# Softmax shift through one 24-column transpose and three row transfers, auxiliary ring of five tasks

## The reference

```python
xn = _layernorm(x, axis=-1)
s = _L0_attn_ref(xn, ...)          # softmax over keys, floored at 1e-10, times v, out projection
g = _silu(_L0_ffn_ref(xn, ...))    # router top-4, silu(gate)*up, down, plus a shared expert
x = x + s * g
```

## Time and profile before

| | |
|---|---|
| median of three runs | 728.79 us (726.35 to 729.39) |
| the profiled execution | 730.4 us, span 728.2 us |
| PE busy / VectorE / ScalarE / POOL | 634.6 / 485.3 / 462.1 / 331.5 us |
| DMA engines' mean busy share, queue of SP | 30.9% |
| transposes of the shift (L764) | 256 |
| copies of the shift (L1227) | 32 |

### The profile page before, as it was taken

How to read it: one execution, slowest core, us unless ns; L and a number is a source line. 1 busy time by engine, 2 the same in 40 slices (tenths; PEclk the granted TensorE clock), 3 DMA queues, 4 the chain that set the end, 5 groups by cost and what they waited for, 6 DMA issues and landing times.

```text
span 728.2 us, 18937 instructions
## 1 busy us (share of the span) xinstructions
PE 634.6 (87%) x5458; PEld 449.4 (62%) x5458; DVE 485.3 (67%) x973; ACT 462.1 (63%) x1082; POOL 331.5 (46%) x691
## 2 busy tenths in 40 slices
PE   2299699966899989999999899899989999998992
PEld 1194256943666666666666666666667666766651
DVE  5939742036777688677777867867787777775265
ACT  1532752036887777787777778777777887785311
POOL 5600677774344433444454344344434444543124
PEclk9979898556999999999999999999999999999996
DMA  8970465500034333333433323333332333321562
GB/s 258 148 245 0 139 160 143 132 0 13 28 82 99 93 80 74 77 82 82 95 89 84 73 73 83 82 83 85 103 74 73 78 82 82 78 55 30 194 201 86
DMA packets 76852, 69.45 MB, mean 95 GB/s; under 512 B 15938, under 2 KB 67204, under 8 KB 76820
## 3 DMA queue, kind: packets, MB, share of 16 engines
q1 hardware_dynamic: 68596, 60.51, 30.9%
q0 software_dynamic: 8224, 8.54, 6.4%
HBM read 47.88 MB, written 21.17 MB: 95 GB/s over the span
## 4 chain that ended last, share of the span: by engine, by line
PE 65%; DVE 14%; ACT 9%; issue 7%; DMA 3%; SPq 0%; ACTq 0%; POOL 0%; DVEq 0%; POOLq 0%
PE PSB L721 8%; PE PSB L696 7%; PE PSB L822 7%; PE PSB L814 6%; PE PSB L740 6%; PE PSB L786 5%; PE PSB L796 5%; PE PSB L743 5%; DVE NEGM L1216 4%; ACT PB L984 4%; ACT PSB L975 3%; PE PSB L670 3%; PE PSB L655 2%; PE PSB L642 2%; PE PSB L672 2%
## 5 line engine op out<-in xcount | busy, mean ns | idle before, releaser
L1216 DVE TENSOR_REDUCE NEGM<-PSB 128x1 f32<-128x1024 f32 (+7 forms) x256 | 192.1, 753 | 65.5 <-PE PSB L698 64.6
L984 ACT ACTIVATE PB<-PSB 128x128 f32<-128x128 f32 (+7 forms) x256 | 165.9, 649 | 39.5 <-PE PSB L723 34.3
L975 ACT ACTIVATE PSB<-PSB,NEGM 128x1024 f32<-128x1024 f32 (+7 forms) x256 | 182.9, 714 | 11.7 <-DVE NEGM L1216 10.7
L1222 DVE TENSOR_SCALAR PB<-PB 128x128 f32<-128x128 f32 (+7 forms) x256 | 118.9, 473 | 60.0 <-ACT PB L984 56.1
L721 PE MATMUL PSB<-STACKS 111*128 111x512 bf16 (+3 forms) x384 | 105.7, 330 | 20.4 <-ACT PSB L975 12.4
L696 PE MATMUL PSB<-STACKS 111*128 111x512 bf16 (+3 forms) x384 | 109.9, 343 | 10.3 <-ACT PSB L975 9.6
L1427 POOL DMA_INDIRECT slot_table<-XE,DI x64 | 66.6, 1040 | 60.3 <-DVE DI L1193 41.1
L1483 POOL DMA_INDIRECT moe_rows<-YE,IDX x32 | 52.9, 1654 | 45.6 <-issue 45.6
L740 PE MATMUL PSB<-PB,VH 128*32 128x256 f32 x640 | 67.3, 383 | 0.0
L743 PE MATMUL PSB<-PB,VH 128*32 128x128 f32 x1024 | 61.5, 276 | 0.0
L721 PEld LDWEIGHTS PSB<-STACKS 111*128 111x128 bf16 x384 | 29.4, 98 | 50.6 <-ACT PB L984 20.5
(11 more groups left out here) (189 smaller groups left out, 1344.6 us busy)
## 6 DMA issues: line engine op xcount, KB each, us to landing
STACKS<-q_parts SPq DMA_DIRECT2D x192, 32.0 KB
STACKS<-k_parts SPq DMA_DIRECT2D x192, 32.0 KB
WG<-in_L_ffn_w_gate_dram SPq DMA_DIRECT2D x32, 176.0 KB
WU<-in_L_ffn_w_up_dram SPq DMA_DIRECT2D x32, 176.0 KB
WD<-in_L_ffn_w_down_dram SPq DMA_DIRECT2D x32, 176.0 KB
q_parts<-PB SPq DMA_DIRECT2D x8, 384.0 KB, 2.6
k_parts<-PB SPq DMA_DIRECT2D x8, 384.0 KB, 3.1
XN<-in_L_attn_qkv_dram SPq DMA_DIRECT2D x4, 512.0 KB, 6.2
```

What stands on the lines that cost most here:

```text
L975: act.activation(sc, sc, ACT.Exp, bias=NEGM[:, par, i:i + 1], accum_out=LSUM[:, par, i:i + 1]).then_inc(exp1_done, 1)
L984: act.activation(PB[:, k % 2, prob_offset(s):prob_offset(s) + (s + 1) * P], psf[:, base:base + (s + 1) * P], ACT.Exp).then_inc(exp2_done, 1)
L1216: dve.tensor_reduce(NEGM[:, par, i:i + 1], psf[:, base:base + (i + 1) * P], AX_X, ALU.max, negate=True).then_inc(max_ready, 1)
L1222: dve.tensor_scalar(p, p, FLOOR, None, ALU.max).then_inc(clamp_done, 1)
```

## The change

1. The shift's parts are stored part by part, `C3[P, 3, NQ]`. One transpose of 24 columns (a 128 x 24 operand) puts 24 rows of 128 into columns 256 and up of `O_BANK`, at step 5 instead of step 7; it waits for the chain, for the copy before it and for the heads' evacuation.
2. VectorE copies them into a new tile `CT[24, 128]` at step 5 (`turn_shift`), and three transfers on SP's queue (`store_shift`), each from eight partitions of 256 bytes into one row of 2 KB, put them into the query stack. They stand at the end of SP's work for a unit. `c_rows_ready` counts 48 per unit.
3. The ring has five tasks, SA, TR, GU, SB, DN. SA stays at steps 2 and 3, TR moves from step 1 to step 3 (ScalarE's copy from step 2 to step 4), GU from steps 4 and 5 to 5 and 6, SB's part 0 from 6 to 7, DN stays. ScalarE's and VectorE's part of GU moves from step 6 to 7, the evacuation of heads from 4 to 3.
4. `values` also waits for the copy of the shift, POOL's chain for that copy instead of the rows, and `DST2` shares the space of `PK`.

```diff
-TR, SA, GU, SB, C, DN = range(6)
-AUX_TASKS = 6
+SA, TR, GU, SB, DN = range(5)
+AUX_TASKS = 5
+C_COL = 256
...
-        C3 = sb("C3", [P, NQ, 3], BF16)
+        C3 = sb("C3", [P, 3, NQ], BF16)
+        CT = sb("CT", [3 * NQ, P], BF16)
...
                 store_heads(it, k - 1)
+                store_shift(it, k + 1)
+
+            def store_shift(it, k):
+
+                hold(sp, c_turned, unit(it, k, 1, 1))
+                rows = QS[k % SLOTS]
+                for a in range(3):
+                    sp.dma_start(rows[SHIFT + a:SHIFT + a + 1, :].rearrange("o (t q) -> o t q", q=P),
+                                 CT[NQ * a:NQ * a + NQ, :]).then_inc(c_rows_ready, 16)
...
+            store_shift(0, 0)
+            store_shift(0, 1)
...
-                    pe.wait_ge(c_rows_ready, unit(it, k, 1, 1))
+                    pe.wait_ge(c_rows_ready, unit(it, k, 48, 48))
...
+                    pe.wait_ge(c_turned, UNITS if is_last(it, k) else unit(it, k, 1, 2))
...
-            def c_transpose(o, ready, parts_count):
-
-                pe.wait_ge(c_parts_ready, parts_count)
-                for i in range(NQ):
-                    ins = pe.transpose(o[SHIFT:SHIFT + 3, i * P // 2:(i + 1) * P // 2].bitcast(BF16),
-                                       C3[:, i, :], IDB[:, :])
-                ins.then_inc(ready, 1)
+            def c_transpose(it, k):
+
+                pe.wait_ge(c_parts_ready, unit(it, k, 1, 1))
+                if k >= 1:
+                    pe.wait_ge(c_turned, unit(it, k))
+                    pe.wait_ge(o_evacuated, unit(it, k, 1, -1))
+                pe.transpose(PSB[0:3 * NQ, O_BANK, C_COL:C_COL + P // 2].bitcast(BF16),
+                             C3[:, :, :].rearrange("p a t -> p (a t)"), IDB[:, :]).then_inc(c_flipped, 1)
...
-                    if s == 1:
-                        if not first:
-                            expert_down(it, k - 1, *aux_begin(it, k - 1, DN))
-                        expert_transpose(it, k, *aux_begin(it, k, TR))
-                    if s == 7 and not last:
-                        c_transpose(*aux_begin(it, k, C), unit(it, k, 1, 2))
-                    if s in (2, 3):
-                        shared(it, k, SA, s - 2, last)
-                    if s in (4, 5):
-                        expert_up(it, k, s - 4, last)
-                    if s == 6:
-                        shared(it, k, SB, 0, last)
+                    if s == 1 and not first:
+                        expert_down(it, k - 1, *aux_begin(it, k - 1, DN))
+                    if s in (2, 3):
+                        shared(it, k, SA, s - 2)
+                    if s == 3:
+                        expert_transpose(it, k, *aux_begin(it, k, TR))
+                    if s == 5 and not last:
+                        c_transpose(it, k + 1)
+                    if s in (5, 6):
+                        expert_up(it, k, s - 5)
+                    if s == 7:
+                        shared(it, k, SB, 0)
...
-                    if s == 2:
-                        o = aux_task(it, k, ix(TR))
+                    if s == 4:
+                        shared(it, k, SA)
+                        o = aux_task(it, k, TR)
                         act.activation(XET[:, :, :].rearrange("p c m -> p (c m)"), o[:, 0:D], ACT.Copy)\
                             .then_inc(xet_ready, 1)
-                    if s == 4:
-                        shared(it, k, ix(SA), SA)
-                    if s == 6:
-                        tanh_gate(it, k, ix(GU), GU, FE)
+                    if s == 7:
+                        tanh_gate(it, k, GU, FE)
...
-                dve.wait_ge(aux_ready[b], count)
-                dve.tensor_copy(QS[k % SLOTS][SHIFT:SHIFT + 3, :], PSB[SHIFT:SHIFT + 3, AUX + b, :].bitcast(BF16))\
-                    .then_inc(c_rows_ready, 1)
+            def turn_shift(it, k):
+
+                dve.wait_ge(c_flipped, unit(it, k, 1, 1))
+                if k >= 1:
+                    dve.wait_ge(c_rows_ready, unit(it, k, 48))
+                dve.tensor_copy(CT[:, :], PSB[0:3 * NQ, O_BANK, C_COL:C_COL + P // 2].bitcast(BF16))\
+                    .then_inc(c_turned, 1)
```

More of the change, by code:

```diff
@@ L745, in values, with aux_begin @@
                 ins.then_inc(pv_done, 1)
[L747 to L752, removed]
+            def aux_begin(it, k, task):
+                if task >= 2:
+                    pe.wait_ge(*aux_done(it, k, task - 2))
                 elif k >= 1:
[L754 to L757, removed]
+                    pe.wait_ge(*aux_done(it, k - 1, task + AUX_TASKS - 2))
+                b, _ = aux(it, k, task)
                 return PSB[:, AUX + b, :], aux_ready[b]
-            def c_transpose(o, ready, parts_count):
-                pe.wait_ge(c_parts_ready, parts_count)
-                for i in range(NQ):
-                    ins = pe.transpose(o[SHIFT:SHIFT + 3, i * P // 2:(i + 1) * P // 2].bitcast(BF16),
-                                       C3[:, i, :], IDB[:, :])
-                ins.then_inc(ready, 1)
+            def c_transpose(it, k):
[5 more added lines that the diff above has]
+                             C3[:, :, :].rearrange("p a t -> p (a t)"), IDB[:, :]).then_inc(c_flipped, 1)
             def expert_transpose(it, k, o, ready):
@@ L797, in expert_down, with shared @@
                 ins.then_inc(ready, 1)
-            def shared(it, k, task, part, last):
+            def shared(it, k, task, part):
                 slot, which = k % SLOTS, 0 if task == SA else 1
-                b, _ = aux(it, k, aux_index(task, last))
+                b, _ = aux(it, k, task)
                 o, ready = PSB[:, AUX + b, :], aux_ready[b]
                 if part == 0:
-                    aux_begin(it, k, task, last)
+                    aux_begin(it, k, task)
                 if slot < 3:
@@ L839, in phase @@
                     if s == 0 and not first:
-                        shared(it, k - 1, SB, 1, False)
+                        shared(it, k - 1, SB, 1)
                     pass2(it, k, s, ahead)
@@ L1005, in tanh_gate, with shared @@
                     .then_inc(tanh_ready, 1)
-            def shared(it, k, a, task_):
+            def shared(it, k, task_):
                 which = 0 if task_ == SA else 1
@@ L1010, in shared @@
                 if slot < 3:
-                    tanh_gate(it, k, a, task_, FSZ[2 * slot + which])
+                    tanh_gate(it, k, task_, FSZ[2 * slot + which])
                 else:
-                    o = aux_task(it, k, a)
+                    o = aux_task(it, k, task_)
                     t = turn(it, k, SLOTS, 2, which)
@@ L1023, in _, with weigh @@
                         exp_seed(0, 0)
-            def weigh(it, k, last):
-                o = aux_task(it, k, aux_index(DN, last))
+            def weigh(it, k):
+                o = aux_task(it, k, DN)
                 act.wait_ge(idx_ready, unit(it, k, 1, 1))
@@ L1273, in phase @@
                 last = is_last(it, k)
-                ix = lambda t: aux_index(t, last)
                 for s in range(NQ):
@@ L1280, in phase @@
                     if s == 0 and not first:
-                        shared(it, k - 1, SB, SB)
+                        shared(it, k - 1, SB)
                         clamp(it, k - 1, NQ - 1)
-                    if s == 4 and not first:
+                    if s == 3 and not first:
                         evacuate_heads(it, k - 1)
                     if s == 4:
-                        shared(it, k, ix(SA), SA)
-                    if s == 6:
+                        shared(it, k, SA)
+                    if s == 5 and not last:
+                        turn_shift(it, k + 1)
+                    if s == 7:
                         if not first:
@@ L1291, in phase @@
                             dve.wait_ge(aux_ready[b], before + 1)
-                        silu_up(it, k, ix(GU), GU, HE[:, :, :].rearrange("p f c -> p (f c)"), FE)
-                    if s == 7 and not last:
-                        b, before = aux(it, k, C)
-                        c_rows(it, k + 1, b, before + 1)
+                        silu_up(it, k, GU, HE[:, :, :].rearrange("p f c -> p (f c)"), FE)
             def gated_output(g):
```

56 lines of the change are left out of this document (27 added, 29 removed).

## The result

The changed kernel takes **745.34 us** (median of four runs, 740.99 to 747.27) against 727.96 for the kernel before. The ratio is 1.0244, with a 95% interval of 1.0215 to 1.0273. That is slower, outside the predicted range, and on the side of rival 1. The profiled execution of after took 740.99 us, with a span of 739.2, at the fast end of its runs; so differences between profiles come out up to 4 us smaller than differences between medians.

The account below looks back on a forecast made before the run. PE was taken to bound the kernel, with ScalarE setting its pace in mid-unit. 728.8 - 1.5 (ring, transposes) + 0.7 (late rows) + 1.2 (start) - 0.9 (last units) = 728.3, rounded to 728 us; range 718 to 740.

Parts of the forecast that it names:

- rival 1: SP's queue becomes the clock at step 0's second pass: 736 us with landing 2.0, 745 with 2.4; chance 0.20.
- The circle of SP: From step 0's second pass through SP's loads, heads, transfers and landing to the next such pass: 15.4 us.
- first step that failed: SP's three new transfers, costed like the four bare head stores at 0.43 us per issue.
- The ring and the transposes: Reordered ring tasks and fewer transposes together: 0.2 us a period gained, between -0.6 and +0.9; 1.5 us in all.
- second step that failed: End of a unit: seven fewer transposes on PE save 0.47 us a unit.
- one of them is 0.07: One small transpose on PE, at the end of a unit, was taken as 0.07 us.
- Step 5: With the gate product moved behind it, step 5's second pass waits for step 4's exponential: PE stands 0.75 us every unit.
- Step 7: Before step 7's second pass PE's wait goes from 0.30 to 0.24 us, new in slot 3.
- Rival 3: The expert's tanh before step 7's largest exponential adds 0.2 to 0.37 us a unit: 734 to 739 us; chance 0.08.
- Some 0.2 us returns: First half: PE reaches step 2 before step 0's exponential is done, giving back 0.2 of the 0.56 us gained.
- The down product's wait: The expert's down product no longer waits 0.40 us for VectorE (0.56 with the load before it) in slots 1 to 3.
- The start and the end: Uncovered copy, issues and landing at the start cost 1.2 us or more; the last two units gain 0.9 us.

Follow-up runs that it names:

- the first four kernels: Changed kernel with transfers ahead of heads (734.89 us), one transfer for three (735.90), no shift transfers (735.16), or the ring's old order (734.25).
- without rows: Changed kernel without the shift transfers and the waits for them, so the softmax is unnormalized: 735.16 us.
- The run with one transpose: Kernel before with one of its eight small transposes kept, VectorE's copy reading that block eight times: 723.14 us.
- the late gate: Old ring order with one early transfer (717.72 us), but expert gate and up products at steps 5 and 6, tanh and product at 7: 730.67 us.
- the 717.7 us version: Changed kernel with the ring's work in the old order, and the three rows in one transfer issued ahead of the heads: 717.72 us.

## Why the prediction was wrong

The measured loss of 17 us has two parts. The medians of the first four kernels give about 10 us for the late rows (745.3 against 735.2 without them) and about 8 us for ring and transposes (735.2 against 726.8). The profiled executions give the rows 5.8 us (spans 739.2 and 733.4). By the starts of SP's loads the units from 191.72 to 641.52 in after, and from 193.15 to 634.75 without rows, take 449.8 and 441.6 us. So the rows cost 8.2 us there: 0.9 in the first three units, 3.6 in the period behind them, and 0.7 to 0.8 in each of the five periods after that. The stretches before and behind were 2.4 us shorter in after, which is not explained.

**The circle of SP: right mechanism, wrong sizes.** The prediction put it at 2.3 + 11.6 + 1.5 = 15.4 us and called that "just what a unit of slots 0 to 2 takes". Measured in the chain above:

- From the second pass of step 0 to SP's start, 459.26 - 456.98 = 2.28. Right.
- From there to the third issue, 471.36 - 459.26 = 12.10, for 11.6. The **first step that failed** is "four bare issues took 1.72, so 0.43 each": the new issues follow each other at 0.76 and 0.68 us, 1.44 for two and not 0.86. That is the whole half microsecond.
- Landing 1.69, for 1.5, and 0.12 behind it.

Together that is 16.2 us. A unit of slots 0 to 2 without rows takes 15.56 to 15.81. The prediction put 0.1 us a period on the lateness; in the steady loop it costs 0.76. Rival 1 named the place, the circle and the direction, and said that it decides once a landing takes over 1.7 us. It decided at 1.69, because the issues had used up the slack first. The bounds of the prediction stretched the landing (1.3 to 2.4) and never the issue, although the issue had the same lack of a row: each issue in the loop read or wrote HBM. The 0.15 us of lateness of the forecast became waits of 0.22 and 0.57 in the two units above, and PE waits 12.9 us in all, 21 times.

**The ring and the transposes: both halves off.** Predicted was a net gain of 0.2 us a period, inside bounds of 0.6 lost to 0.9 gained; measured is a loss of 0.95, just past the lower bound. Per unit, from the trace without rows:

| | predicted | measured |
|---|---|---|
| first half, slots 1, 2, 3, 0 | 0.5, 0.5, 0.36, 0 gained | 0.74, 0.74, 0.56, 0.23 gained |
| second half, slots 0 to 2 | 0.22 lost | 0.69 to 0.75 lost |
| second half, slot 3 | 0.52 lost | 1.04 lost |

The first half runs from the first matmul of step 0 to the second pass of step 4, the second half from there on.

- "Seven give 0.47 us a unit, bare on PE": **the second step that failed**, and the one most off in the ring's sum. The run with one transpose shows 0.20. Eight hold PE for 0.54 us, but 0.34 of it are there with one transpose too. A start-to-start distance is not what a removal gives, when what stands behind would have had to wait anyway.
- The one transpose, "one of them is 0.07": at its new place between full-width matmuls it takes from 465.31 to 465.62, 0.31, where the same neighbours stood 0.06 apart (458.09 to 458.15 in the trace of before). It costs 0.25. With the 0.27 above, that is 0.5 us in each unit's second half, about the whole difference in the table.
- Step 5, "PE stands 0.75 us in every unit": right. The next second pass came 1.30 us after the last, where the prediction had 1.29. As a piece by itself the late gate is worth 13 us.
- Step 7, "it now waits 0.24": measured as the prediction measured its 0.30, it is 0.15 (468.13 + 0.06 to 468.34), a little less than forecast. Rival 3's tanh at that place costs nothing that shows.
- "Some 0.2 us returns" in the first half: this is not seen. In slot 3 the whole 0.56 came. In slot 1 the start of the down product moved 0.54 us nearer to the second pass of step 1, that pass came 0.08 sooner, and the wait before step 4 fell from 0.51 to 0.41. In slot 0, where nothing was forecast, that wait fell from 0.51 to 0.30, nearly all of the 0.23. So 0.9 us a period were won that the prediction did not count, and hid nearly half of the 2.0 that it missed in the second halves.
- The down product's wait is gone in all variants, as predicted, and the 717.7 us version gains in the first half, where that wait stood: in slots 1 and 2 it takes 8.48 and 8.64 us where before took 8.93 and 9.08. Its second half is 0.08 longer there.

**The start and the end.** The prediction gave the start 1.2 us. After's first full period, 242.48 to 311.34 by the starts of SP's loads, is 68.86 us long, 2.8 above the steady one. In the run without rows the same stretch, 242.97 to 308.27, takes its usual 65.3. The three units before it take 50.76 us in after and 49.82 without rows. So the late rows cost 0.9 us in those three units and 3.6 in the first full period, where the forecast had 1.2 for the whole start. The 0.9 us that the last two units were to gain were not tested by themselves.

## What to carry over

A queue is part of the loop as soon as its last instruction feeds the next round. Add its circle up from trigger to use, bound each kind of issue that has no row, and put what others wait for ahead of stores that nobody waits for; here two swapped lines are worth 10 us. Where two engines alternate, keep a filler between each pair of dependent steps. And before counting a removed instruction at the distance it holds, ask what stands behind it and whether that could have started. Two costs that hide each other, like the circle and the ring here, show their size only when both are removed: the ring alone gave 11 us, the rows alone 10, both 28.

## Not expected of the hardware

- An issue on SP of 2 KB from SBUF to SBUF, eight partitions to one, holds the queue 0.635 us (median of 96), twice the 0.33 of a 16 KB head store, while one of 6 KB from 24 partitions to three takes 0.78. So the hold does not go with the bytes alone. What sets it was not tested.
- The landing of the small transfer, 1.69 us, lies between the head stores with an empty queue (1.4 to 1.5) and those behind the loads (2.3 to 2.4).
- Narrow stationary operands among full-width ones cost a gap on each side: the transpose of 24 columns starts 0.15 us behind its neighbour and its successor 0.16 behind it, where 0.06 is usual, and the load of full-width weights behind the values of 32 columns waits 0.20 to 0.41 us for nothing that the trace names (L824 at 470.38 and 460.53 in after, among the waits above). The Trainium skill, "TensorEngine Tiling (Array Packing)", Key Properties, says that changing the tiling mode drains TensorE, and gives no duration. The gaps stand where the operand goes from narrow to full width and back, and they would be explained by it. No run here varies the mode alone, so this stays an attribution. The prediction did not weigh that rule.
